# Transformer layer on one core: the fourth and later background tasks of a slot move between the two halves of its PV products

## The chip, the cores and the metric

One core of one Trainium2 chip runs the whole kernel as one launch. The metric is the device time of that launch in microseconds (us); lower is better. Before the change three runs gave 1093.54, 1095.59 and 1097.42 us, median 1095.59 us.

## The reference

The kernel computes one pre-norm layer on an input of 2048 tokens of width 128, all in float32: causal attention with 16 heads of width 64, then a mixture of eight experts (top 2) and one shared expert. Only the attention is touched. Cut to what matters:

```python
qkv = einsum('bse,ehd->bshd', layernorm(x), qkv_w) + qkv_b      # 16 heads, 3*64 each
logits = einsum('bqhd,bkhd->bhqk', q, k) / sqrt(64)             # causal mask: where(tril, logits, -big)
probs = softmax(logits)
attn = einsum('bhqk,bkhd->bqhd', probs, v)
x = x + einsum('bqhd,hde->bqe', attn, out_w) + out_b
x = x + shared_ffn(layernorm(x)) + routed_ffn(layernorm(x))     # 8 experts, top 2, hidden width 352
```

## The kernel before, in words

**Attention.** The 2048 queries of a head are four blocks of 512, its keys 16 tiles of 128. A *group* (b, p) is query block b against the two key tiles 2p and 2p+1, as far as the causal mask leaves any; there are 2+4+6+8 = 20 groups in a head (`GROUPS`), 320 in all. For a group TensorE (PE) computes the transposed scores into PSUM (`scores`, L827 and L828, and L832, which adds the mask on a diagonal tile), ScalarE (ACT) takes the exponential twice, once in float32 and once in float16 (L503, L504), GpSimd (POOL) subtracts the two to get the float16 remainder `p_lo` (L420), and PE multiplies both float16 parts with the values (`p_times_v`, L852, L854, L856). This last step is the "PV products": for each of the two key tiles (k = 0, 1) and each of up to four query tiles, three products of 64 or 65 columns in float16. So a full key tile gives 12 products and a diagonal one 3 to 12. The scores are products in float32 (`float32r`) of up to 512 columns.

**Slots.** PE's instructions are written out in one fixed order. Each head has 20 *slots*, one for each group. In slot n PE issues the first background task, the scores of the group's first key tile, the second background task, the scores of its second key tile, all the other background tasks of the slot, and then the PV products of the group three slots earlier (`LAG = 3`): first k = 0, then k = 1. Semaphore waits stand at the head of a product's weight load: the PV products of k = 0 wait for `p_lo`, and, where they begin a new query block, for `attn_ready`, by which VectorE (DVE) says that it has read the previous block's sums (`normalise`, L654 and L656). After k = 1 they count up `p_used`, which `normalise` and a later exponential wait for.

**Background tasks.** They prepare the next head and finish the last pair of heads, and all go through a ring of three PSUM banks `bg` (`BGRING = 3`): PE fills a bank, DVE drains it, and the task k waits until task k-3 is drained (`bg_drained`). The kinds are "qk" (three products of 512 columns, L743 to L745), "v" (L783), "att_t" (L803), "att_y" (L743 to L745), "shift" (L798), and "max": one float32 product of query tile t against key block c, 128 to 512 columns wide (L793), of which DVE takes the row maximum (L632, or L628 on the diagonal). The row maxima of a head are needed only at "shift", in slot 18 of the head before.

**The planner.** `background(h)` writes the slots at build time: fixed places for qk (slots 0 to 3), v, att_t, att_y and shift, and `fill` spreads the 40 max tasks of a head over the slots 4 to 17, by an estimate of what DVE needs for each. Run for all 16 heads, its lists have 83 slots with four tasks or more: 76 with four and 7 with five. By slot number these 83 are: slot 4 in 8 heads (in 7 of them with five tasks), slot 6 in 8, slot 7 in 14, slot 8 in 7, slot 10 in 6, slot 11 in 13, slot 12 in 6, slot 13 in 8, slot 14 in 13. The head 15 has none. Every fourth and fifth task is a "max": 90 tasks. In the 8 slots numbered 13 the third task is 128 columns wide and the fourth 512.

The ends of the order: before the slots a prologue prepares head 0 (until about 58 us of the span), head 15 runs from about 767 us, and a second layer norm and nine passes over expert weights end the kernel.

Of the kernel before, what the change touches and what calls it, by code (L numbers as in the profile page):

```python
# [52 lines left out]
def max_width(t, c):  # L53
    return min(BLK, P * (t + 1) - BLK * c)
# [26 lines left out]
def background(h):  # L81


    i, s = divmod(h, 2)
    slots = [[] for _ in range(NG)]
    if s == 0 and i:
        slots[ATT_LAST[0]].append(("att_t", i - 1, 3))
        slots[ATT_LAST[1]].append(("att_y", i - 1, 3))
    if s == 1:
        for b in range(NB - 1):  # L90
            slots[ATT_SLOTS[b][0]].append(("att_t", i, b))
            slots[ATT_SLOTS[b][1]].append(("att_y", i, b))
    if i + 1 < PAIRS:
        for k in range(2):
            slots[V_SLOTS[s][k]].append(("v", i + 1, 2 * s + k))
    if h + 1 < H:
        for b in range(NB):
            slots[b].append(("qk", h + 1, b))
        taken = [sum(map(vector_time, slot)) for slot in slots]
        for n in range(NG):  # L100
            if ends_block((n - LAG - 1) % NG):
                taken[n] += 0.6
        level = 1.5
        while True:
            trial = [list(slot) for slot in slots]
            if fill(trial, max_tasks(h + 1), [max(level - x, 0.1) for x in taken]):
                break
            level += 0.02
        slots = trial
        slots[SHIFT_SLOT].insert(0, ("shift", h + 1))  # L110
    return slots
# [5 lines left out]
SLOTS = [background(h) for h in range(H)]  # L117
# [6 lines left out]
def wait(eng, sem, value):  # L124

    if not isinstance(value, int) or value > 0:
        eng.wait_ge(sem, value)


def layer_kernel(nc, x_t, qkv_w, qk_bias_in, v_bias, out_w, out_bias, gate_w_t, ffn_w, out_t):  # L130
    ctx = ExitStack()
    with ctx:
# [129 lines left out]
        def blk(b):  # L262
            return slice(b * BLK, (b + 1) * BLK)

        def tile(t):
            return slice(t * P, (t + 1) * P)

        def drained(task):

            return NUMBER[task] + 1  # L270
# [469 lines left out]
        def _(pe):  # L740
            def mm3(out, w_hi_ap, w_lo_ap, x_hi_ap, x_lo_ap, start, stop, skip=False):

                nc.tensor.matmul(out, w_hi_ap, x_hi_ap, start=start, stop=False, skip_group_check=skip)  # L743
                nc.tensor.matmul(out, w_hi_ap, x_lo_ap, start=False, stop=False, skip_group_check=skip)  # L744
                return nc.tensor.matmul(out, w_lo_ap, x_hi_ap, start=False, stop=stop, skip_group_check=skip)  # L745
# [22 lines left out]
            def background_task(task):  # L768
                k = NUMBER[task]
                bank = bg[:, k % BGRING]  # L770
                wait(pe, bg_drained, k - BGRING + 1)
                if task[0] == "qk":
                    h, b = task[1:]
                    ws, s = h // 2 % 2, h % 2
                    if b == 0:
                        pe.wait_ge(w_lo_ready, h // 2 + 1)
                    mm3(bank, w_hi[ws][:, s], w_lo[ws][:, s], xn_hi[:, blk(b)], xn_lo[:, blk(b)], True, True
                        ).then_inc(bg_ready, 1)
                elif task[0] == "v":
                    i, q = task[1:]  # L780
                    pe.wait_ge(w_landed[i % 2], (i // 2 + 1) * 32)
                    for r in range(4):
                        mm = nc.tensor.matmul(bank[:, tile(r)], xn[:, tile(4 * q + r)], w_raw[i % 2][:, :, 2 * D:3 * D],  # L783
                                              start=True, stop=True)
                    mm.then_inc(bg_ready, 1)
                elif task[0] == "max":
                    h, t, c = task[1:]
                    s = h % 2
                    if t % 4 == 0 and c == 0:
                        pe.wait_ge(q_hi_landed[t // 4], (h + 1) * 32)  # L790
                        pe.wait_ge(k_lo_landed[t // 4], (h + 1) * 16)
                    width = max_width(t, c)
                    mm = nc.tensor.matmul(bank[:, 0:width], q_hihi[s][:, tile(t)],  # L793
                                          k_lohi[s][:, c * BLK:c * BLK + width], start=True, stop=True)
                    mm.then_inc(bg_ready, 1)
                elif task[0] == "shift":
                    pe.wait_ge(neg_max_ready, task[1] + 1)
                    nc.tensor.transpose(bank[0:NT, 0:P], neg_max[:], ident[:]).then_inc(bg_ready, 1)  # L798
                elif task[0] == "att_t":
                    i, b = task[1:]  # L800
                    pe.wait_ge(attn_ready, (i * 2 + 1) * NB + b + 1)
                    for r in range(4):
                        mm = nc.tensor.transpose(bank[:, tile(r)], attn[:, 4 * b + r, :], ident[:])  # L803
                    mm.then_inc(bg_ready, 1)
                elif task[0] == "att_y":
                    i, b = task[1:]
                    pe.wait_ge(wo_lo_ready, i + 1)
                    pe.wait_ge(bg_drained, drained(("att_t", i, b)))
                    mm3(bank, wo_hi[i % 2][:], wo_lo[i % 2][:], att_hi[:], att_lo[:], True, True).then_inc(bg_ready, 1)
# [27 lines left out]
            def p_times_v(h, n, k):  # L837

                b, p = GROUPS[n]
                B, (i, s) = h * NB + b, divmod(h, 2)  # L840
                if k == 0:
                    if n == 0 and s == 0:
                        pe.wait_ge(bg_drained, drained(("v", i, 3)))
                    if p == 0:
                        wait(pe, attn_ready, B)
                    pe.wait_ge(p_lo_ready, h * NG + n + 1)
                kt = 2 * p + k
                v = v_parts[i % 2][:, s, kt]
                for j in range(max(0, kt - 4 * b), 4):
                    out = pv4[:, j, :]  # L850
                    cols = slice(k * BLK + j * P, k * BLK + (j + 1) * P)
                    nc.tensor.matmul(out, p_hi[:, n % PRING, cols], v[:, 0:D + 1],  # L852
                                     start=(kt == 0 and j == 0), stop=False, skip_group_check=True)
                    nc.tensor.matmul(out[:, 0:D], p_hi[:, n % PRING, cols], v[:, D + 1:VW],  # L854
                                     start=False, stop=False, skip_group_check=True)
                    mm = nc.tensor.matmul(out, p_lo[:, n % PRING, cols], v[:, 0:D + 1],  # L856
                                          start=False, stop=(kt == 4 * b + j), skip_group_check=True)
                if k == 1:
                    mm.then_inc(p_used, 1)
# [15 lines left out]
            for h in range(H):  # L875
                for n in range(NG):
                    for task in SLOTS[h][n][0:1]:
                        background_task(task)
                    scores(h, n, 0)
                    for task in SLOTS[h][n][1:2]:  # L880
                        background_task(task)
                    scores(h, n, 1)
                    for task in SLOTS[h][n][2:]:
                        background_task(task)
                    m = (n - LAG) % NG
                    if m < n or h:
                        for k in range(2):
                            p_times_v(h if m < n else h - 1, m, k)
            for n in range(NG - LAG, NG):
                for k in range(2):  # L890
                    p_times_v(H - 1, n, k)
# [95 lines left out]
```

## Time and profile before

| | before |
|---|---|
| median of 3 runs | 1095.59 us |
| profiled execution, its own time | 1095.27 us |
| its span, first to last instruction | 1093.5 us |
| PE products (MATMUL) busy | 1050.8 us, 96% |
| PE weight loads (PEld) busy | 867.1 us, 79% |
| DVE, ACT, POOL busy | 799.5, 784.8, 757.2 us |
| TensorE clock granted, mean | 0.973 |

The rows below are from this one profiled execution. PE's products are pipelined, and the end of each is modelled: a row's duration is longer than the time until the next product may start. What the array really spends on a product is read from one start to the next; rows of the timeline give starts to 0.01 us. PEld is the weight load that precedes each product.

### The profile page before, as it was taken

Reading aid. Unit: us, or ns where it says so; the run is one execution under the profiler, and the core shown is the slowest. Engines: PE = TensorE matmul, PEld = TensorE weight load, DVE = VectorE, ACT = ScalarE, POOL = GpSimd, SP = SyncE. Lnnn points to the kernel's source line nnn. Section 1 sums busy time; section 2 is a strip of 40 time slices with the busy share of each in tenths; the row PEclk is TensorE's granted clock in tenths of the full one; section 3 lists DMA queues with packets and bytes.
Section 4 is the critical chain, followed back from the end, with each engine's and each line's share of the span. In section 5 each row is a group of like instructions: output and inputs, shape, how many; then the busy total and the mean of one; then the engine's idle time right before and its main releaser. Section 6 shows DMA issues by size and latency. Waiting matters only on the chain.

```text
span 1093.5 us, 25737 instructions
## 1 busy us (share of the span) xinstructions
PE 1050.8 (96%) x10580; PEld 867.1 (79%) x10580; DVE 799.5 (73%) x1659; ACT 784.8 (72%) x952; POOL 757.2 (69%) x427
## 2 busy tenths in 40 slices
PE   7889999999999999999999999999976999999998
PEld 5478888888888888888888888888855677777776
DVE  5976878787787878778787787878225577777765
ACT  3068787878878787887878888788952656666664
POOL 2058878888878887887888788788970556555540
PEclk9689999999999999999999999999986999999999
DMA  2330312303032130312303031130100311111001
GB/s 83 67 78 6 75 38 50 79 2 86 11 69 61 26 80 2 86 25 56 71 16 79 2 86 38 44 75 6 46 1 1 107 76 61 60 60 60 39 1 38
DMA packets 24653, 53.22 MB, mean 49 GB/s; under 512 B 5720, under 2 KB 8024, under 8 KB 22488
## 3 DMA queue, kind: packets, MB, share of 16 engines
q1 hardware_dynamic: 24544, 51.68, 18.3%
q8 instruction: 80, 1.31, 0.5%
q14 instruction: 29, 0.24, 0.1%
HBM read 16.86 MB, written 1.11 MB: 16 GB/s over the span
## 4 chain that ended last, share of the span: by engine, by line
PE 71%; POOL 11%; issue 6%; DVE 5%; DMA 4%; ACT 2%; SPq 0%; POOLq 0%; ACTq 0%; DVEq 0%
PE bg L793 13%; PE st L827 11%; PE st L828 11%; PE pv L852 6%; PE pv L854 6%; PE pv L856 6%; POOL xw L442 4%; POOL p_lo L420 3%; PE bg L743 3%; DMA attn<-comb_dram 3%; PE bg L783 2%; POOL k_lohi L447 2%; PE bg L744 2%; PE bg L745 2%; POOL q_lo_shift L434 2%
## 5 line engine op out<-in xcount | busy, mean ns | idle before, releaser
L420 POOL TENSOR_TENSOR p_lo<-prob,p_hi 128x1024 f16<-128x1024 f32 x320 | 617.1, 1946 | 156.3 <-ACT p_hi L504 154.5
L503 ACT ACTIVATE prob<-st,p_bias 128x1024 f32<-128x1024 f32 x320 | 330.3, 1032 | 126.5 <-PE st L828 100.5
L504 ACT ACTIVATE p_hi<-st,p_bias 128x1024 f16<-128x1024 f32 x320 | 328.4, 1026 | 0.0
L632 DVE TENSOR_REDUCE row_max<-bg 128x1 f32<-128x512 f32 x384 | 255.6, 686 | 16.0 <-PE bg L793 10.8
L827 PE MATMUL st<-q_hihi,k_lohi 128*128 128x512 f32 (+3 forms) x640 | 245.7, 384 | 2.7 <-DMA q_lo_shift<-shift_row 1.4
L852 PEld LDWEIGHTS pv<-v_parts,p_hi 128*128 128x128 f16 x2176 | 197.6, 96 | 58.0 <-issue 39.4
L793 PE MATMUL bg<-k_lohi,q_hihi 128*128 128x512 f32 (+3 forms) x640 | 239.9, 406 | 3.4 <-DVE v_parts L622 2.1
L852 PE MATMUL pv<-v_parts,p_hi 128*128 128x65 f16 x2176 | 236.2, 194 | 2.2 <-POOL p_lo L420 2.2
L828 PE MATMUL st<-q_lo_shift,k_hi_one 65*128 65x512 f32 (+3 forms) x640 | 235.6, 368 | 0.0
L854 PE MATMUL pv<-v_parts,p_hi 128*128 128x64 f16 x2176 | 233.7, 195 | 0.0
L856 PE MATMUL pv<-v_parts,p_lo 128*128 128x65 f16 x2176 | 231.9, 192 | 0.0
L856 PEld LDWEIGHTS pv<-v_parts,p_lo 128*128 128x128 f16 x2176 | 202.9, 99 | 0.0
L854 PEld LDWEIGHTS pv<-v_parts,p_hi 128*128 128x128 f16 x2176 | 202.6, 97 | 0.0
L793 PEld LDWEIGHTS bg<-k_lohi,q_hihi 128*128 128x128 f32 x640 | 122.0, 194 | 29.7 <-DVE row_max L632 7.7
L827 PEld LDWEIGHTS st<-q_hihi,k_lohi 128*128 128x128 f32 x640 | 122.4, 191 | 17.7 <-ACT p_hi L504 2.3
L828 PEld LDWEIGHTS st<-q_lo_shift,k_hi_one 65*128 65x128 f32 x640 | 121.7, 190 | 16.7
L727 DVE TENSOR_TENSOR prob<-prob,st 128x512 f32<-128x512 f32 x108 | 73.9, 684 | 72.9 <-ACT prob L548 72.4
L548 ACT ACTIVATE prob<-st 128x512 f32<-128x512 f32 x108 | 64.5, 597 | 67.0 <-PE st L745 67.0
L612 DVE TENSOR_SCALAR k_lohi<-bg,qk_bias 128x512 fp32r<-128x512 f32 x64 | 48.0, 750 | 72.4 <-PE bg L745 72.3
L442 POOL TENSOR_TENSOR xw<-xn,attn 128x512 f32<-128x512 f32 x32 | 51.2, 1611 | 62.3 <-DMA attn<-comb_dram 61.0
L628 DVE CUSTOM_DVE_ANT_0 xw<-bg,mask_wide 128x512 f32<-128x512 f32 (+2 forms) x169 | 79.0, 474 | 7.6 <-PE bg L793 7.4
L434 POOL TENSOR_TENSOR q_lo_shift<-e_raw,k_hi_one 128x1152 fp32r<-128x1152 f32 x9 | 24.8, 2750 | 60.5 <-ACT k_hi_one L527 60.5
(147 smaller groups left out, 1643.8 us busy)
## 6 DMA issues: line engine op xcount, KB each, us to landing
q_hihi<-k_lohi SPq DMA_DIRECT2D x128, 128.0 KB, 2.3
k_lohi<-q_lo_shift SPq DMA_DIRECT2D x64, 128.0 KB, 2.3
k_hi_one<-k_lohi SPq DMA_DIRECT2D x16, 512.0 KB, 4.3
attn<-comb_dram SPq DMA_DIRECT2D x8, 1024.0 KB, 4.4
e_raw<-ffn_w SPq DMA_DIRECT2D x9, 576.0 KB, 5.4
w_raw<-qkv_w SPq DMA_DIRECT2D x8, 192.0 KB, 2.3
res<-x_t SPq DMA_DIRECT2D x4, 256.0 KB, 3.8
out_t<-xn SPq DMA_DIRECT2D x4, 256.0 KB, 2.5
```

What stands on the lines that cost most here:

```text
L420: nc.gpsimd.tensor_tensor(o, a, b, ALU.subtract).then_inc(p_lo_ready, 1)
L442: nc.gpsimd.tensor_tensor(xw32[:, b % 2], xn[:, blk(b)], w_tok[:, blk(b)], ALU.mult).then_inc(xw_ready, 1)
L503: nc.scalar.activation(o32, src, ACT.Exp, bias=p_bias[:], scale=D ** -0.5)
L504: nc.scalar.activation(o16, src, ACT.Exp, bias=p_bias[:], scale=D ** -0.5).then_inc(exp_done, 1)
L628: nc.vector.tensor_tensor_reduce(masked[k % BGRING][:, 0:width], bank[:, 0:width], mask_wide[:, BLK - width:BLK], 1.0, -3.0e38, ALU.add, A ...
L632: nc.vector.tensor_reduce(row_max[:, t, c:c + 1], bank, AX_X, ALU.max).then_inc(bg_drained, 1)
L793: mm = nc.tensor.matmul(bank[:, 0:width], q_hihi[s][:, tile(t)], k_lohi[s][:, c * BLK:c * BLK + width], start=True, stop=True)
L827: nc.tensor.matmul(out, k_lohi[s][:, tile(kt)], q_hihi[s][:, q], start=True, stop=False)
L828: mm = nc.tensor.matmul(out, k_hi_one[s][0:D + 1, tile(kt)], q_lo_shift[s][0:D + 1, q], start=False, stop=not diagonal)
L852: nc.tensor.matmul(out, p_hi[:, n % PRING, cols], v[:, 0:D + 1], start=(kt == 0 and j == 0), stop=False, skip_group_check=True)
L854: nc.tensor.matmul(out[:, 0:D], p_hi[:, n % PRING, cols], v[:, D + 1:VW], start=False, stop=False, skip_group_check=True)
L856: mm = nc.tensor.matmul(out, p_lo[:, n % PRING, cols], v[:, 0:D + 1], start=False, stop=(kt == 4 * b + j), skip_group_check=True)
```

## The change

In each slot the tasks from the fourth on are issued between the PV products of k = 0 and those of k = 1, and no longer ahead of both. A slot with three tasks or fewer keeps its order. DVE, ACT, POOL and the DMA queue keep their programs: DVE drains the banks in the same order as before, since the order of the background tasks among themselves is unchanged.

```diff
                     scores(h, n, 1)
-                    for task in SLOTS[h][n][2:]:
+                    for task in SLOTS[h][n][2:3]:
                         background_task(task)
                     m = (n - LAG) % NG
                     if m < n or h:
-                        for k in range(2):
-                            p_times_v(h if m < n else h - 1, m, k)
+                        p_times_v(h if m < n else h - 1, m, 0)
+                    for task in SLOTS[h][n][3:]:
+                        background_task(task)
+                    if m < n or h:
+                        p_times_v(h if m < n else h - 1, m, 1)
```

## Rows read from the trace of the kernel before

**Rows 1.** The page: share of the span and instructions; the chain that ended last.
```profile
PE 1050.8 (96%) x10580; PEld 867.1 (79%) x10580; DVE 799.5 (73%) x1659; ACT 784.8 (72%) x952; POOL 757.2 (69%) x427
PE 71%; POOL 11%; issue 6%; DVE 5%; DMA 4%; ACT 2%; SPq 0%; POOLq 0%; ACTq 0%; DVEq 0%
```
**Rows 2.** Windows, all engines (stretch, its length, busy us of each, PEclk, DMA share, GB/s).
```profile
320.00:384.00 64.00, 64.00 (x777) 54.19 (x775) 52.52 (x116) 51.35 (x54) 52.03 (x29) 1.00 0.16 38
...
64.00:767.20 703.20, 702.56 (x8701) 597.57 (x8701) 553.83 (x1246) 577.50 (x612) 582.88 (x312) 1.00 0.21 48
```
**Rows 3.** Waits of the weight loads, 109 to 755 us (us in total, times, longest).
```profile
PEld pv L852 <- issue: 33.4, 147, 0.3
PEld pv L852 <- POOL p_lo L420: 8.8, 34, 0.3
PEld bg L793 <- DVE row_max L628: 0.3, 1, 0.3
```
**Rows 4.** Waits of the weight loads for drained max banks, whole span.
```profile
PEld bg L793 <- DVE row_max L632: 7.7, 22, 0.5
...
PEld bg L793 <- DVE row_max L628: 2.8, 10, 0.5
```
**Rows 5.** Timeline of PE, head 5, slot 11 and the start of slot 12 (start, us).
```profile
323.06 0.27 PE L832 MATMUL st<-mask_cols_r,ident_r 128*128 128x128 f32 x1
323.17 0.67 PE L793 MATMUL bg<-k_lohi,q_hihi 128*128 128x512 f32 x2
323.69 0.20 PE L852 MATMUL pv<-v_parts,p_hi 128*128 128x65 f16 x1
...
323.79 0.19 PE L852 MATMUL pv<-v_parts,p_hi 128*128 128x65 f16 x1
...
324.07 0.19 PE L852 MATMUL pv<-v_parts,p_hi 128*128 128x65 f16 x1
...
324.43 0.48 PE L743 MATMUL bg<-att_hi,wo_hi 128*128 128x512 f32 x1
324.75 0.39 PE L744 MATMUL bg<-att_lo,wo_hi 128*128 128x512 f32 x1
324.98 0.40 PE L745 MATMUL bg<-att_hi,wo_lo 128*128 128x512 f32 x1
```
**Rows 6.** Products of the qk tasks, whole span (count, busy us, mean ns of one).
```profile
L743 PE MATMUL bg<-xn_hi,w_hi 128*128 128x512 f32 x64 | 30.9, 482 | 0.9 <-DVE xn_lo L584 0.5 <-DVE q_lo_shift L614 0.4
L744 PE MATMUL bg<-xn_lo,w_hi 128*128 128x512 f32 x64 | 25.8, 403 | 0.0
```
**Rows 7.** Timeline of PE, head 5, first task of slot 4, which follows PV products.
```profile
304.43 0.31 PE L793 MATMUL bg<-k_lohi,q_hihi 128*128 128x128 f32 x1
304.57 0.45 PE L827 MATMUL st<-q_hihi,k_lohi 128*128 128x512 f32 x1
```
**Rows 8.** Timeline of PE, head 7, slot 4 and the start of slot 5.
```profile
400.54 0.85 PE L793 MATMUL bg<-k_lohi,q_hihi 128*128 128x384 f32 x3
...
401.50 0.19 PE L856 MATMUL pv<-v_parts,p_lo 128*128 128x65 f16 x1
401.59 1.16 PE L783 MATMUL bg<-w_raw,xn 128*128 128x128 f32 x8
```
**Rows 9.** Timeline of DVE, the same stretch.
```profile
400.97 0.56 DVE L628 CUSTOM_DVE_ANT_0 xw<-bg,mask_wide 128x384 f32<-128x384 f32 x1 [0.21 <-PE bg L793]
401.45 0.08 DVE L628 DVE_READ_ACCUMULATOR2_ANT row_max<- 128x1 f32 x1
```
**Rows 10.** Timeline of PE, head 5, slot 13, third and fourth task.
```profile
329.51 0.51 PE L793 MATMUL bg<-k_lohi,q_hihi 128*128 128x128 f32 x2
```
**Rows 11.** Timeline of DVE, head 5, slots 13 and 14.
```profile
330.11 0.69 DVE L632 TENSOR_REDUCE row_max<-bg 128x1 f32<-128x512 f32 x1
331.03 1.39 DVE L632 TENSOR_REDUCE row_max<-bg 128x1 f32<-128x512 f32 x2 [0.23 <-PE bg L793]
```
**Rows 12.** Timeline of POOL, head 5, groups 8 and 9.
```profile
318.79 4.24 POOL L420 TENSOR_TENSOR p_lo<-prob,p_hi 128x1024 f16<-128x1024 f32 x2 [0.96 <-ACT p_hi L504]
```

## The prediction

> **What bounds the kernel now.** I read the page first. PE's products are busy for 96% of the span and PE holds 71% of the chain that ended last; no other engine has more than 11% of it [rows 1]. A busy share is an average over stages, and PE's ends are modelled, so the windows come next. In a stretch of attention PE is busy for all 64.00 of 64.00 us, with the clock at 1.00, while DVE has 52.52, ACT 51.35 and POOL 52.03; over all the slots of heads 0 to 14 it is 702.56 of 703.20 us [rows 2]. The reader is to see that nothing but PE's own stream can be late there by much. The waits say the same. Between 109 and 755 us the weight loads waited for a drained max bank once, for 0.3 us [rows 3]; the larger sums for the whole span, 7.7 and 2.8 us [rows 4], therefore belong nearly all to the prologue, where PE fills banks as fast as DVE drains them. The two big entries, 33.4 and 8.8 us before the first PV load, are 181 pieces of at most 0.3 us, 0.23 us on average [rows 3]. The timeline shows what they are: the PV load stands behind a running float32 product of 512 columns, and the PV product starts when that product's turn is over. It is PE work beside an idle load port and not lost time.
>
> So the change is to be priced on PE's stream, from start to start. A float32 product of 512 columns behind another wide one takes 0.23 us (324.75 to 324.98), and a full key tile of PV products 0.38 us for 12 (323.69 to 324.07) [rows 5].
>
> **The change part by part.** No instruction is added or removed; 90 max products in 83 slots move behind the PV products of k = 0. What changes are PE's neighbours. Before: ... third, fourth, PV0, PV1, next slot. After: ... third, PV0, fourth (and fifth), PV1, next slot. The stream now goes from float16 products to a float32 product once more in each of the 83 slots, and from float32 to float16 once more.
>
> (1) *Float16 to float32, a cost.* The first float32 product after PV products takes 0.32 us to the next start (324.43 to 324.75), against 0.23 for the one behind it [rows 5]. Over all 64 qk tasks the first product has 482 ns, the second 403, so 79 ns more [rows 6]; most of these first products stand behind PV products. A narrow one pays the same: 128 columns, which at the wide product's pace are 0.06 us, took 0.14 (304.43 to 304.57) behind PV products [rows 7]. The load of float32 weights is longer than the 0.03 us for which a PV product covers it, so its tail lies open. I take 0.08 us. The exact case, a max product behind PV products with its bank drained long before, is in the trace already at the head of slots such as this one. 83 x 0.08 = 6.6 us.
>
> (2) *Float32 to float16, a cost.* The first three PV products after a float32 one take 0.10 us (323.69 to 323.79), against 0.38 / 12 x 3 = 0.095 in the whole tile [rows 5]. Rounded starts allow 0 to 0.02; the longer spans of first products that I looked at favour 0.01. 83 x 0.01 = 0.8 us.
>
> (3) *The narrow neighbour, a gain.* A wide product behind a 128-column one also pays for an open load: third and fourth task behind a mask product took 0.52 us (323.17 to 323.69), which is 0.29 + 0.23 [rows 5]. In the 8 slots numbered 13 the third task is 128 columns wide and the fourth 512 [rows 10]. There this 0.06 goes, since a PV product follows the narrow one: -8 x 0.06 = -0.5 us.
>
> (4) *The bank wait of slot 5, a gain.* In the 7 slots with five tasks the first task of the next slot needs the bank of the third. DVE's last step on that bank is over at 401.45 + 0.08 = 401.53, and PE starts the next task at 401.59, 0.09 after the last PV product instead of 0.03 [rows 8, 9]. With slot 4 itself 0.09 longer, PE comes after the drain: -7 x 0.06 = -0.4 us. The other bank waits of moved tasks are not there to be saved, by the 0.3 us in all [rows 3].
>
> (5) *POOL, nothing.* The PV products of k = 0 come earlier by one max product, 0.23 us, and their wait for `p_lo` with them. In slot 11 of head 5 group 8 is wanted at 323.69 [rows 5]; POOL did groups 8 and 9 in one run from 318.79 to 323.03, so group 8 was ready at about 320.9 [rows 12]: 2.8 us of cover, of which 0.23 goes. `p_used` comes 0.09 us later with the rest of the stream, and ACT, POOL and the loads of the next head are paced by the scores, which keep their place. SP's queue issues nothing inside the moved block.
>
> (6) *DVE, nothing by my reading.* A moved task's bank lands later by PV0 plus the switch, at most 0.38 + 0.09 = 0.47 us. DVE starts 0.43 us after the start of a product when it has been waiting (400.54 to 400.97) [rows 8, 9]. In slot 13 it started the fourth 0.54 us after that product's start (329.57 to 330.11), a backlog of 0.11; the delay for DVE is then 0.36 + 0.07 - 0.06 - 0.11, about 0.3 us [rows 10, 11]. But DVE waits 0.23 us for the next slot's first task there [rows 11], which absorbs it, and the moved bank is wanted again only by the third task after it. In slot 4 with five tasks DVE begins the fourth at 401.53 at the latest, and the fourth product would start at about 400.98 instead of 400.77: no delay.
>
> The sum is 6.6 + 0.8 - 0.5 - 0.4 = 6.5 us. It is on PE's stream in the stretch where nothing else is last, so it moves everything behind it; the head 15, whose end waits for POOL, has no moved task and cannot hide any of it. The profiled execution took 1095.27 us (span 1093.5 and 1.8 outside): 1095.27 + 6.5 = 1101.8. The median of the three runs is 0.3 higher, so I forecast 1102.1 us, 0.6% slower.
>
> *A rule of the Trainium skill that speaks against (1).* The rows show 0.32 against 0.23 us [rows 5]. "TensorE: Matmul & The Clock Gate", section "Step-by-step: what each phase is for", says that TensorE pulls a weight load ahead of the products in flight, so that the next weights load while the current product runs. Taken as full cover, the switch is free and the sum would be -0.5 - 0.4, no change; the rows say that a PV product is too short a cover.
>
> **The rivals.**
> *A. The switch is hidden, no change.* If the load of the moved product is issued early enough behind PV0 (its bank is long free, unlike a slot's first task in some cases), the 0.08 shrinks. For it: the load port has idle time. Against: the qk and max tasks at slot heads, whose banks are also free, pay 0.08 as a rule [rows 5 to 7]. From full to no cover the time is 1094.7 to 1102.1; with half of it 6.5 - 3.3 = 3.2, 1098.8.
> *B. Faster: the ring of three banks.* The fourth task needs the first's bank, and 0.38 us of PV products now stand in front of it. If the 10.5 us of waits for drained max banks [rows 4] lay in these slots, they would go: 1095.6 - 10.5 + 6.5 = 1091.6. It decides as soon as a moved task waited over 0.09 us before. Against: 0.3 us in the stretch that holds nearly all of them [rows 3].
> *C. Slower by more: DVE late.* If the 0.3 us of slot 13 reaches PE (through the next slot's banks or `attn_ready`), 8 slots cost another 0.2 each beyond PE's own delay, and some 0.06 in the 13 slots 14: 1.6 + 0.8 = 2.4, 1104.5. For it: slot 4 to 5 of head 7 shows that such a chain can be tight [rows 8, 9]. Against: DVE's slack of 11 us in 64 [rows 2] and the 0.23 us of waiting right behind.
> *D. POOL late for the earlier PV products.* If the 34 pieces put down to `p_lo` [rows 3] were real waits, moving them up costs 34 x 0.23 = 7.8: 1109.9. Against: the 2.8 us of cover.
>
> **How the numbers follow.** This kernel's runs differ by up to 0.2% from their median, so about 0.3%, 3.3 us, is what a measurement can tell from no change. Chances: the forecast with its bounds (switch 0.06 to 0.10 in all, 1099.7 to 1103.0, and 1.5 us of measurement on either side) 0.80; A 0.10, mostly inside 0.3%; B 0.03; C 0.05; D 0.02. Faster 0.04, same 0.11, slower 0.85. The range, 1098.5 to 1105.5, takes in C and the upper half of A, and leaves out B, D and the free switch.
>
> **What would show it.** In the changed profile: a moved max product of 512 columns takes 0.31 to 0.32 us to the next start behind PV0 (0.23: A is right); PE still busy for 64.00 of 64.00 us; heads 0 to 14 longer by about 6.5 us and the rest unchanged; the 0.2 to 0.3 us pieces of idle load port before the first PV load grow in number by about 83, of the k = 1 half; waits for `attn` and for `row_max` in 109 to 755 us no larger (larger: C), those for `p_lo` no longer than 0.3 each (longer: D). The prediction is wrong if the time moves without PE's start-to-start intervals around the moved products doing so.

## The result, and the profile after

The changed kernel took 1105.14 us (median of 4 runs, 1104.52 to 1106.62) against 1095.83 for the kernel before, a ratio of 1.0089, 95% interval 1.0068 to 1.0109. Timed again beside the experiments it took 1104.51 against 1097.57, a ratio of 1.0063 (1.0045 to 1.0082). It is slower by 7 to 9 us, where 6.5 us, a ratio of 1.0059, were forecast: inside the second interval and below the first. 1105.14 us lies in the forecast's range, near its upper edge.

The page of the changed kernel answers to [rows 1]: PE holds the same share of the chain, and its busy time has grown by 11.1 us.

```profile
PE 1061.9 (96%) x10580; PEld 870.9 (79%) x10580; DVE 804.7 (73%) x1659; ACT 785.4 (71%) x952; POOL 757.6 (69%) x427
PE 71%; POOL 11%; issue 6%; DVE 5%; DMA 4%; ACT 2%; SPq 0%; POOLq 0%; ACTq 0%; DVEq 0%
```

The stages say where. These are windows as in [rows 2], cut at the first product of slot 0, the first score product of head 15 and the last PV product: first the kernel before, then the changed one.

```profile
0.00:30.00 30.00, 22.14 (x117) 16.99 (x117) 17.88 (x28) 9.36 (x18) 9.05 (x20) 0.94 0.34 92
30.00:57.41 27.41, 22.48 (x58) 12.30 (x58) 26.46 (x65) 0.00 (x0) 0.00 (x0) 0.69 0.22 48
57.41:767.60 710.19, 708.10 (x8723) 602.02 (x8722) 556.28 (x1249) 579.90 (x614) 583.27 (x312) 1.00 0.21 48
767.60:810.00 42.40, 38.92 (x579) 32.55 (x579) 8.63 (x17) 39.45 (x43) 42.09 (x24) 0.99 0.07 25
810.00:1093.40 283.40, 259.14 (x1111) 203.20 (x1108) 190.24 (x301) 156.04 (x278) 122.80 (x73) 0.95 0.13 49
```
```profile
0.00:30.00 30.00, 24.36 (x101) 19.29 (x101) 15.07 (x24) 9.37 (x18) 7.98 (x20) 0.77 0.26 74
30.00:60.18 30.18, 24.84 (x75) 14.13 (x74) 29.39 (x69) 0.00 (x0) 1.07 (x1) 0.72 0.28 62
60.18:777.47 717.29, 715.62 (x8723) 602.01 (x8722) 560.26 (x1249) 580.56 (x614) 583.92 (x312) 1.00 0.21 48
777.47:819.70 42.23, 38.72 (x579) 32.37 (x579) 8.64 (x17) 39.45 (x43) 41.89 (x24) 1.00 0.07 26
819.70:1102.70 283.00, 258.33 (x1113) 203.09 (x1109) 191.35 (x301) 156.03 (x278) 122.79 (x73) 0.95 0.13 49
```

The span is 9.2 us longer. Heads 0 to 14 have 7.1 of it (717.29 - 710.19), with the same number of products and the clock at 1.00 in both. The other 2.8 us lie ahead of the first slot, where the two programs issue the same instructions: the mean granted clock of the first 30 us was 0.94 in the one execution and 0.77 in the other. Head 15 and all behind it gave back 0.6.

The traces can be cut finer, at the first product of each slot. Here are heads 1 to 14, changed kernel less the kernel before, once for the two first profiles and once for the second profile of the changed kernel (after_again) less that of the unedited copy (control).

| slots of heads 1 to 14 | number | grew by, us, first pair | second pair |
|---|---|---|---|
| four tasks, not slot 13 | 66 | 6.37 | 6.33 |
| slot 13, four tasks, third one 128 columns wide | 7 | 0.34 | 0.35 |
| slot 13 of head 14, four tasks, third one 512 wide | 1 | 0.09 | 0.09 |
| five tasks (slot 4) | 7 | 0.27 | -0.22 |
| all others, nothing moved | 199 | 0.10 | -0.62 |

The growth sits in the slots with a moved task, 0.097 us by the median of the 66, and hardly anywhere else. Two profiles of the same program differ too: heads 0 to 14 took 1.66 us more in the copy than in the kernel before, but 1.6 of that lie in four single slots, numbered 3 or 4. Differences of whole stretches below about 2 us therefore say little, and differences slot by slot say much more. (The paragraph on the planner, and term (3) of the forecast, give all 8 slots numbered 13 a narrow third task. It is so in 7: in head 14 the second task is the narrow one.)

The timeline of PE in slot 11 of head 5 answers to [rows 5].

```profile
328.13 0.28 PE L828 MATMUL st<-q_lo_shift,k_hi_one 65*128 65x128 f32 x1
328.24 0.27 PE L832 MATMUL st<-mask_cols_r,ident_r 128*128 128x128 f32 x1
328.35 0.44 PE L793 MATMUL bg<-k_lohi,q_hihi 128*128 128x512 f32 x1
328.63 0.20 PE L852 MATMUL pv<-v_parts,p_hi 128*128 128x65 f16 x1
...
328.99 0.19 PE L856 MATMUL pv<-v_parts,p_lo 128*128 128x65 f16 x1
329.01 0.48 PE L793 MATMUL bg<-k_lohi,q_hihi 128*128 128x512 f32 x1
329.34 0.20 PE L852 MATMUL pv<-v_parts,p_hi 128*128 128x65 f16 x1
...
329.69 0.19 PE L856 MATMUL pv<-v_parts,p_lo 128*128 128x65 f16 x1
329.71 0.48 PE L743 MATMUL bg<-att_hi,wo_hi 128*128 128x512 f32 x1
```

From the third task to the next slot's first product are 1.36 us (328.35 to 329.71) instead of 1.26 (323.17 to 324.43). The moved product takes 0.33 to the next start instead of 0.23. Over the 57 moved fourth tasks of 512 columns this interval has a median of 0.321 us.

The waits of the weight loads between 111 and 760 us answer to [rows 3].

```profile
PEld pv L852 <- issue: 40.5, 186, 0.3
PEld pv L852 <- POOL p_lo L420: 5.9, 22, 0.3
PEld pv L852 <- DVE attn L656: 1.6, 6, 0.3
```

The view of [rows 3] has the same line for `attn`, between its second and its third:

```profile
PEld pv L852 <- DVE attn L656: 1.6, 6, 0.3
```

There is no wait for a row maximum. The pieces of idle load port ahead of PV loads are 208 instead of 181, where the forecast looked for 83 more. In total the port's idle time ahead of L852 is 68.1 us instead of 58.0, in the page's table of costliest groups, so it did grow by about 0.12 us a slot, but most of it in pieces that this view does not list. That sign of the forecast failed; it had named the wrong view for it.

### The profile page after: what moved, and what is told of

It reads as the page before. It is cut to its first block, busy times and chain, and to the rows that moved or that the text cites. A ratio compares the mean times of both kernels' runs of the same rounds, so it can differ in the third digit from the quotient of the medians.

```text
span 1102.7 us, 25737 instructions
## 1 busy us (share of the span) xinstructions
PE 1061.9 (96%) x10580; PEld 870.9 (79%) x10580; DVE 804.7 (73%) x1659; ACT 785.4 (71%) x952; POOL 757.6 (69%) x427
## 4 chain that ended last, share of the span: by engine, by line
PE 71%; POOL 11%; issue 6%; DVE 5%; DMA 4%; ACT 2%; SPq 0%; POOLq 0%; ACTq 0%; DVEq 0%
PE bg L793 13%; PE st L827 11%; PE st L828 11%; PE pv L852 6%; PE pv L854 6%; PE pv L856 5%; POOL xw L442 4%; POOL p_lo L420 3%; DMA attn<-comb_dram 3%; PE bg L743 3%; POOL k_lohi L447 2%; PE bg L783 2%; PE bg L744 2%; PE bg L745 2%; POOL q_lo_shift L434 2%
## 5 line engine op out<-in xcount | busy, mean ns | idle before, releaser
L632 DVE TENSOR_REDUCE row_max<-bg 128x1 f32<-128x512 f32 x384 | 255.8, 686 | 18.2 <-PE bg L793 12.8
L793 PE MATMUL bg<-k_lohi,q_hihi 128*128 128x512 f32 (+3 forms) x640 | 258.6, 415 | 3.3 <-DVE v_parts L622 2.1
L852 PEld LDWEIGHTS pv<-v_parts,p_hi 128*128 128x128 f16 x2176 | 197.2, 96 | 68.1 <-issue 47.2
L827 PE MATMUL st<-q_hihi,k_lohi 128*128 128x512 f32 (+3 forms) x640 | 245.8, 384 | 2.5 <-ACT p_hi L504 1.6
L852 PE MATMUL pv<-v_parts,p_hi 128*128 128x65 f16 x2176 | 245.4, 195 | 2.2 <-POOL p_lo L420 2.2
L854 PE MATMUL pv<-v_parts,p_hi 128*128 128x64 f16 x2176 | 242.2, 195 | 0.0
L856 PE MATMUL pv<-v_parts,p_lo 128*128 128x65 f16 x2176 | 240.1, 192 | 0.0
L827 PEld LDWEIGHTS st<-q_hihi,k_lohi 128*128 128x128 f32 x640 | 122.4, 191 | 18.2 <-ACT p_hi L504 2.8
L828 PEld LDWEIGHTS st<-q_lo_shift,k_hi_one 65*128 65x128 f32 x640 | 121.7, 190 | 16.7
L434 POOL TENSOR_TENSOR q_lo_shift<-e_raw,k_hi_one 128x1152 fp32r<-128x1152 f32 x9 | 24.8, 2752 | 59.2 <-ACT k_hi_one L527 59.2
```

The source lines that it names most:

```text
L632: nc.vector.tensor_reduce(row_max[:, t, c:c + 1], bank, AX_X, ALU.max).then_inc(bg_drained, 1)
L827: nc.tensor.matmul(out, k_lohi[s][:, tile(kt)], q_hihi[s][:, q], start=True, stop=False)
L828: mm = nc.tensor.matmul(out, k_hi_one[s][0:D + 1, tile(kt)], q_lo_shift[s][0:D + 1, q], start=False, stop=not diagonal)
```

## Experiments

Each kernel was timed in five rounds beside the kernel before. "Heads 0 to 14" is read in its profiled execution between the same two products as above. The kernel before has 710.19 us in its first profile, its copy 711.85.

| run | ratio to before, 95% interval | heads 0 to 14, us |
|---|---|---|
| control (before, a copy) | 1.0003 (0.9992 to 1.0015) | 711.85 |
| after_again (the change) | 1.0063 (1.0045 to 1.0082) | 717.76 |
| fourth_behind | 1.0020 (1.0007 to 1.0033) | 712.21 |
| third_between | 1.0124 (1.0106 to 1.0141) | 726.91 |
| scores_between | 1.0120 (1.0099 to 1.0141) | 723.01 |
| third_behind | 1.0128 (1.0107 to 1.0149) | 725.13 |
| diagonal_behind | 1.0043 (1.0024 to 1.0062) | 715.72 |
| covered | 1.0085 (1.0067 to 1.0103) | 720.66 |
| beside | 1.0139 (1.0116 to 1.0163) | 725.58 |
| pairs | 1.0098 (1.0079 to 1.0116) | 718.97 |
| pairs_shift | 1.0146 (1.0126 to 1.0166) | 722.78 |
| pairs_spread | 1.0270 (1.0247 to 1.0293) | 742.10 |

The theory is the forecast's: what costs is that PE changes once more from float16 to float32 products, 0.08 us, and back, 0.01, in each of the 83 slots (the switch). The main rival, L, is that the moved tasks reach DVE late and the delay comes back to PE.

**control and after_again: the start.** No edit.

> The kernel before, unedited, as a second copy. The changed kernel was 9.3 us slower, but its heads 0 to 14 only 7.1 us; 2.8 us more lay ahead of the first slot (first slot at 60.2 us instead of 57.4), at a lower granted clock. Theory P1 (start by chance): the time to the first slot varies from one execution to the next by 2 us or more, at different clocks, in this kernel too; the ratio is 1.000. Theory P2 (the start belongs to the program): this copy reaches its first slot at 57.4 us within 0.5 us.

> The changed kernel, unedited, timed beside the others. Switch theory: heads 0 to 14 take 7.1 us more than before again. P1: the first slot starts anywhere between 56 and 61 us, and the whole is slower by 6.5 to 7.1 us plus or minus what the start differs. P2: the first slot starts at 60.2 us within 0.5 us and the whole is 9.3 us slower.

The copy reached its first slot at 59.4 us, against 57.4 in the first profile. The windows of its first 30 us and of the stretch behind the last PV product:

```profile
0.00:30.00 30.00, 23.89 (x106) 18.18 (x107) 15.96 (x25) 9.36 (x18) 8.70 (x20) 0.83 0.29 80
...
813.40:1099.80 286.40, 261.81 (x1115) 205.24 (x1111) 191.13 (x301) 156.06 (x278) 123.13 (x73) 0.94 0.13 48
```

P1 holds: with identical instructions ahead of it, the first slot began between 57.4 and 60.8 us over the 14 profiled executions (12 different kernels), and what follows the last PV product took 283.1 to 287.3. The kernel before alone ran from 1095.49 to 1101.17 us in 23 runs of one session. The changed kernel reached its first slot at 59.2 us this time, and the difference to before was 6.9 us, with 717.76 us in heads 0 to 14.

**fourth_behind: no extra switch, and the banks later still.** Against the changed kernel:

```diff
                     if m < n or h:
-                        p_times_v(h if m < n else h - 1, m, 0)
+                        for k in range(2):
+                            p_times_v(h if m < n else h - 1, m, k)
                     for task in SLOTS[h][n][3:]:
                         background_task(task)
-                    if m < n or h:
-                        p_times_v(h if m < n else h - 1, m, 1)
```

> The fourth and fifth tasks of a slot stand behind both halves of the PV products. Switch theory: PE goes from float16 to float32 as often as in the kernel before, since the next slot begins with float32 anyway, so heads 0 to 14 take the time of before, within 0.5 us. Theory L (the moved tasks reach DVE late, and that delay comes back to PE): DVE gets them later still, by up to 0.75 us instead of 0.47, so heads 0 to 14 are slower than in the changed kernel, by over 7 us against before.

Heads 0 to 14 took 712.21 us, 0.4 more than the copy of before and 2.0 more than its first profile. The later banks do show as waits:

```profile
PEld pv L852 <- DVE attn L656: 4.7, 20, 0.3
PEld bg L783 <- DVE row_max L628: 1.8, 7, 0.3
PEld bg L793 <- DVE row_max L632: 1.2, 7, 0.2
```

These are its load waits between 110 and 755 us. `attn` has 20, against 6 in the kernel before and in the changed one, and two kinds of bank waits are new. But with the switches gone most of the 7 us are gone, although DVE gets the tasks later than in the changed kernel; L asked for more than 7. The total is 0.2% over before, by an interval that leaves out 1. Whether these waits make it or the scatter of starts and ends is not shown.

**third_between: twice the switches.** Against the changed kernel:

```diff
-                    for task in SLOTS[h][n][2:3]:
-                        background_task(task)
...
-                    for task in SLOTS[h][n][3:]:
+                    for task in SLOTS[h][n][2:]:
```

> Already the third task stands between the two halves of the PV products, in all 173 slots that have one, instead of 83. Switch theory: 173 extra switches in each direction at 0.08 + 0.01 us, less 0.05 for each of the 52 narrow products that no longer stand ahead of a float32 one: 13.0 us more than before in heads 0 to 14. Theory L: the delay of each bank is what counts; banks of third tasks are drained with the same slack as fourth ones, so the cost grows with the 173 to at least 7.1 x 2.1 = 14.8 us, with waits of PE for drained banks or attn of over 1 us in all.

Heads 0 to 14 took 15.1 us more than the copy, 16.7 more than the first profile. This run does not decide between the theories. The switches make 13.0 by the forecast's price, and L had asked for at least 14.8 us with waits of over 1 us, which are there: `attn` 26 times with 7.4 us of idle load port, and 1.9 us for `row_max`. Cut by slots, the 161 slots of heads 1 to 14 with a third task grew by 14.5 us against the copy, 0.096 by the median, and most of them lie near 0.05 (narrow neighbours) or 0.1; only slot 9 has 0.15 on average. That is what a fixed price with some waits on top looks like, but it is the next run that tells the two apart.

**scores_between: switches without any task moved.** Against the kernel before, cut to the new lines:

```diff
+                    early = values and h < H - 1 and len(SLOTS[h][n]) <= 2
+                    if early:
+                        p_times_v(h if m < n else h - 1, m, 0)
                     scores(h, n, 1)
...
```

> No background task moves. In the 124 slots of heads 0 to 14 with at most two tasks, the scores of the second key tile stand between the two halves of the PV products. Switch theory: 124 extra switches in each direction at 0.09 us, less 0.05 for each narrow product that no longer stands ahead of a float32 one, 8.3 us in all, and the rows show 0.31 to 0.32 us from the start of the first score product behind PV0 to the next. Theory L (late banks at DVE are what costs): no bank comes later against its neighbours than before, so heads 0 to 14 take the time of before within 1 us.

Heads 0 to 14 grew by 11.2 to 12.8 us, where L says under 1. The timeline shows the price at the moved products, 0.31 us to the next start and 0.23 behind it:

```profile
311.01 0.19 PE L856 MATMUL pv<-v_parts,p_lo 128*128 128x65 f16 x1
311.04 0.48 PE L827 MATMUL st<-q_hihi,k_lohi 128*128 128x512 f32 x1
311.35 0.39 PE L828 MATMUL st<-q_lo_shift,k_hi_one 65*128 65x512 f32 x1
311.58 0.20 PE L852 MATMUL pv<-v_parts,p_hi 128*128 128x65 f16 x1
```

By the forecast's prices 8.3 us are the 124 switches. The trace puts the growth where the switches are: the 119 slots of heads 1 to 14 with at most two tasks took 10.8 us more than in the copy, the other 161 slots 0.0. The median of the 119 is 0.086 us. Eight slots numbered 5 hold 2.4 us of it, up to 0.39 each; they begin a query block, and `attn` is waited for 13 times here (3.9 us of idle load port) instead of 6. A wait for a transfer of `k_lohi` also shows.

**third_behind and diagonal_behind: the narrow neighbours, and a try at a faster kernel.** Tasks from the third on behind both halves, in all slots or only where the second scores end with a mask product (the condition in this diff, cut to its end, which third_behind lacks), against the kernel before:

```diff
+                    if diagonal:
+                        for task in SLOTS[h][n][2:]:
+                            background_task(task)
```

> The third and all later tasks stand behind both halves of the PV products, in 173 slots. Switch theory: as many switches as in the kernel before; only narrow products that stood ahead of a float32 one now stand ahead of PV products, 45 x 0.05 = 2.2 us less in heads 0 to 14, minus what new waits for attn in slot 5 take (0.14 us in each odd head with the fourth task behind): -2.2 to 0 us. Theory L: slower than before by over 2 us, since every bank in these slots comes later by 0.3 to 0.75 us.

> A version meant to beat both kernels: only in the slots whose second scores end with a mask product (52 slots with three tasks or more) do the third and later tasks stand behind both halves of the PV products. Switch theory: the mask product of 128 columns then stands ahead of PV products, which need no open float32 load: 52 x 0.05 = 2.6 us less in heads 0 to 14, no extra switch. Theory L: slower, by 0.3 us or more in each of the slots, or no gain.

Both failed: -2.2 to 0 and -2.6 us were expected. There is no additional switch, yet heads 0 to 14 took 725.13 and 715.72 us, 13.3 and 3.9 more than in the copy. The load waits of third_behind between 110 and 782 us name the place:

```profile
PEld pv L852 <- DVE attn L656: 10.6, 29, 0.5
PEld bg L793 <- DVE row_max L632: 9.6, 33, 0.4
...
PEld bg L783 <- DVE row_max L628: 3.8, 6, 0.6
```

These are idle times of the load port and not lost time one for one. Third, fourth and the next slot's tasks now stand close together, and a ring of three banks lets PE run at most three tasks ahead of DVE. So L names a true limit of this kernel, and the change stayed on the free side of it. That the waits make the whole 13.3 us is argued from their size; no run takes them away alone.

**covered and beside: what the 0.08 us are.** One more float16 product of 252 columns in each of the 83 slots of the changed kernel, ahead of the moved tasks (covered) or behind them (beside). The diff is that of beside, against the changed kernel:

```diff
+                    if SLOTS[h][n][3:]:
+                        nc.tensor.matmul(pv[:, 260:512].rearrange("p (a c) -> p a c", a=2),
+                                         p_hi[:, m % PRING, 3 * P:4 * P],
+                                         v_parts[(h if m < n else h - 1) // 2 % 2][:, 0, 0:2, 0:126],
+                                         start=False, stop=False, skip_group_check=True)
```

> The changed kernel with one more float16 product of 252 columns in each of its 83 slots, between PV0 and the moved task; it writes PSUM columns that nobody reads. The question is what the 0.08 us of the switch are. Open-load theory: the float32 load takes about 0.11 us and only the product before it covers it; behind a product of 0.107 us (252 columns at the pace of a PV product's 65 in 0.029) it is covered, so the pair costs 0.107 - 0.08 = 0.03 us a slot: heads 0 to 14 take 717.5 + 2.4 = 719.9 us, and the moved product takes 0.23 us to the next start. Fixed-price theory (each change of type costs 0.08 whatever stands before it): 717.5 + 83 x 0.107 = 726.4 us, and the moved product takes 0.31 to 0.32.

> The same extra product of 252 columns, but behind the moved tasks, as the first of the k = 1 half, where it covers only a float16 load. Both theories: 83 x 0.107 = 8.9 us more than the changed kernel in heads 0 to 14, 726.4 us, and the moved product still takes 0.31 to 0.32 us to the next start. It is the price of the product alone, for comparison with the run before.

Against after_again the same product cost 7.8 us behind the moved tasks (725.58 - 717.76) and 2.9 ahead of them (720.66 - 717.76); by the ratios 8.3 and 2.4. So about 5 of its 8 us vanish where a float32 load follows, as the open-load theory said. Slot by slot, where the scatter drops out, it is clearer: over the 66 slots with four tasks the product cost 0.105 us behind the moved task and 0.032 ahead of it, so 0.073 of the switch's 0.08 are hidden. A price of the change of type that is paid whatever stands ahead of it is ruled out. That it is the weight load which is covered, and not some other delay of the same length, is supported by products that change no type: of 128 columns each and all float32, they stand 0.11 us apart (328.13, 328.24 and 328.35 in the changed kernel's slot 11), where one of 128 columns behind a wide float32 product takes 0.06 by the median.

But the row that both theories pointed to did not behave. Here is PE at a moved task of 128 columns in the covered kernel, and at one of 512 columns in beside:

```profile
320.90 0.19 PE L856 MATMUL pv<-v_parts,p_lo 128*128 128x65 f16 x1
320.93 0.27 PE L889 MATMUL pv<-v_parts,p_hi 128*128 128x252 f16 x1
320.96 0.31 PE L793 MATMUL bg<-k_lohi,q_hihi 128*128 128x128 f32 x1
321.11 0.21 PE L852 MATMUL pv<-v_parts,p_hi 128*128 128x65 f16 x1
```
```profile
320.62 0.48 PE L793 MATMUL bg<-k_lohi,q_hihi 128*128 128x512 f32 x1
320.94 0.28 PE L891 MATMUL pv<-v_parts,p_hi 128*128 128x252 f16 x1
321.06 0.19 PE L852 MATMUL pv<-v_parts,p_hi 128*128 128x65 f16 x1
```

The product of 252 columns takes 0.12 us to the next start in beside, and 0.03 in covered, where the float32 product behind it still takes its long 0.15 (0.14 in [rows 7]); over all 64 moved tasks of 512 columns in covered it is 0.32, not the 0.23 expected. The record starts the float32 product 0.03 us after whatever float16 product stands before it. So at a switch a single start-to-start interval is not the time of one product; the sum over the switch is what counts, and 0.03 + 0.32 is the 0.105 of this product and the 0.23 of the next, within 0.02.

**pairs, pairs_shift, pairs_spread: half the switches.** The PV products of two groups together, in even slots only. pairs_shift issues slot 18's background tasks behind them; pairs_spread also the fourth and fifth tasks of the even slots. The diff is that of pairs, against the kernel before:

```diff
-                    m = (n - LAG) % NG
-                    if m < n or h:
-                        for k in range(2):
-                            p_times_v(h if m < n else h - 1, m, k)
-            for n in range(NG - LAG, NG):
+                    if n % 2 == 0:
+                        for m in (n - 4, n - 3):
+                            if m >= 0 or h:
+                                for k in range(2):
+                                    p_times_v(h if m >= 0 else h - 1, m % NG, k)
+            for n in range(NG - 4, NG):
```

> The kernel before with the PV products of two groups issued together, in even slots only (groups n-4 and n-3 in slot n). PE goes from float16 to float32 158 times instead of 316. Switch theory: 158 x 0.09 = 14.2 us less, and narrow neighbours give back 1.2: 13 us less, 697 us for heads 0 to 14, if no new wait arises. Theory L (banks and scores late at DVE and ACT bound the order): tasks and scores of two slots now follow one another without PV products in between, and PE waits for drained banks or for exp as in the kernel with all later tasks behind; then over half of the 13 us are lost, and it may be slower than before.

> The kernel with PV products in pairs of groups, and in slot 18 its background tasks (the shift, which waits for the last row maximum) behind the PV products. In the paired kernel the shift's wait took 8.8 of the 20 us by which heads 1 to 14 were longer than their products ask. If the rest stays, 719.0 - 8.8 = 710 us for heads 0 to 14: the kernel before, no gain. If the waits for banks shrink too once DVE is less behind, down to 705. If the later shift row makes the next head's first scores wait (its DMA takes 1.9 us), 712 or more.

> As pairs_shift, and in the even slots the fourth and fifth tasks stand behind the PV products. No switch is added. If late banks at DVE are what eats the gain of the halved switches, the PV products between the third and the fourth task give DVE up to 0.75 us and heads 0 to 14 take 2 to 5 us less than pairs_shift. If it only moves the crowd of tasks into the next slot, the same or more.

No version beats the kernel before. The load waits of pairs between 111 and 776 us:

```profile
PEld bg L798 <- DVE row_max L628: 12.3, 14, 1.1
PEld bg L793 <- DVE row_max L632: 10.4, 34, 0.4
...
PEld bg L743 <- DVE row_max L632: 2.9, 7, 0.4
```

These are 25.6 us of idle load port. Heads 0 to 14 took 718.97 us, where 697 were expected if no wait arose: the new waits cost about 20 us, more than the 13 saved. With the shift behind the PV products its wait is gone, but the next head's scores find ACT late (11.6 us of idle load port ahead of L827 for `p_hi`), and the sum is higher; spreading the tasks made it worse still, where 2 to 5 us less had been one expectation and the same or more the other. By slots, slot 0 of heads 1 to 14, with those scores, took 13.5 us more in pairs_shift than in pairs and 17.8 us more in pairs_spread. The rest of the 23 us between pairs_spread and pairs is not separated.

## Why the prediction was right in its mechanism, and off in size

**What bounds the kernel.** Right. The stretch stayed dense in PE, and the only engine whose program changed is the one that got longer.

**(1) and (2), the switch.** Right, slightly too small. 0.09 us a slot were put in. The 66 slots with four tasks outside slot 13 grew by 0.097 each by the median, and slot 11 of head 5 shows 0.10 (1.36 against 1.26). Over 83 slots that is 0.6 us more than forecast. scores_between shows that the price needs no background task, and covered against beside that most of it can be hidden behind a longer product.

The Trainium skill ("TensorE: Matmul & The Clock Gate", "Step-by-step: what each phase is for") says that the next weights load while the current product runs. Covered against beside agrees, with 0.073 us hidden behind the longer product. The forecast was right not to read it as full cover: behind a product of 65 columns the switch still cost 0.097.

**(3), the narrow neighbour.** The gain is there, smaller and in one slot fewer. Seven slots 13 have a narrow third task, and they grew by 0.048 us instead of 0.097: 0.05 each, not 0.06, and 0.3 us in all instead of 0.5. Slot 13 of head 14, without it, grew by 0.09. The kernels built to collect more of this gain lost it to waits.

**(4), the bank wait of slot 5.** Right in place and size. Five of the seven slots with five tasks grew by 0.03 us in both pairs of profiles, 0.09 less 0.06; the other two, in heads 5 and 11, scatter by more than that. Behind it a small wait moved. DVE is done with `attn` in head 7 at 408.87 + 0.42 = 409.29 us, and PE, no longer held up by the bank, now comes to it a little too early: from the mask product to the first PV product are 0.15 us (409.20 to 409.35), where before there were 0.12. The slot as a whole did not get longer by it: slot 5 changed by -0.01 us in the sum of the seven odd heads.

```profile
408.87 0.42 DVE L656 TENSOR_TENSOR attn<-pv,rden 128x256 f32<-128x256 f32 x1
```
```profile
409.20 0.27 PE L832 MATMUL st<-mask_cols_r,ident_r 128*128 128x128 f32 x1
409.35 0.20 PE L852 MATMUL pv<-v_parts,p_hi 128*128 128x65 f16 x1
```

**(5) and (6), POOL and DVE.** Right. The waits for `p_lo` stayed at 0.3 us at the longest, no wait for a row maximum appeared, and those for `attn` are 6, as before. DVE met the moved task of slot 11 at 329.53, 0.52 us after its product's start, without a stall at PE.

**The rivals.** A (the switch hidden) is out by the slot's own rows. B (faster by the ring of banks) is out: there was nothing to save, as [rows 3] said. C did not happen here: the slots 14, for which it had a delay, grew by 0.096 like the others. It is the limit that fourth_behind touches and third_behind and pairs run into. D did not happen.

**How the numbers followed: the step that failed.** The 6.5 us were sound: heads 0 to 14 grew by 7.1 us, of which 0.6 are the switch at 0.097 instead of 0.09. What failed is the step from there to a time, "How the numbers follow": the base of 1095.59 us, the median of three runs (1095.27 of the profiled one and 0.3), and the 1.5 us allowed for measurement on either side of 1099.7 to 1103.0. 1105.14 lies 2.1 above 1103.0.

The runs showed a wider scatter. In four later sessions the kernel before took 1095.49 to 1101.17 us in 56 runs, with medians from 1097.40 to 1098.61; none of the 56 was as fast as the fastest of the first three, 1093.54. The changed kernel repeated its time, 1104.51 after 1105.14. So the base was some 2 us too low for this kernel, and against 1097.57 the difference is 6.9. The profiles show where such scatter arises. The one behind the forecast had the earliest start of the 14, 57.4 us to the first slot. The stage ahead of the slots moves by 3.4 us from one execution to the next, and the stage behind the last PV product by 4.2. Of the 9.2 us by which the two first spans differ, 7.1 are in heads 0 to 14, 2.8 are the start, and -0.6 the end. Why the first session had so fast a kernel before is not known; four runs are few, and it may be chance.

## What to carry to other kernels

On an engine with no gaps, moving work costs what its new neighbours cost: here 0.1 us each time a float32 product stands behind a float16 one of 65 columns, which is too short to cover its weight load. Count the changes of type in the order before moving anything, and price a move over the whole switch, never by one interval. Look at several runs for the base of a forecast before you give it 1.5 us of room, and compare two profiles slot by slot, where the scatter of the ends drops out. And where a ring of few banks feeds another engine, fewer switches bought by crowding its tasks are paid back with interest.

## What the runs showed of the hardware

A float16 product of 252 columns cost 0.105 us a slot ahead of a float16 load (beside less after, 66 slots) and 0.032 ahead of a float32 load (covered less after): 0.07 us of the load's length were hidden. The same product's row shows 0.12 and 0.03 us to the next start.

The mean clock granted in the first 30 us took four values in 14 executions with the same instructions there. With 0.94 the first slot began at 57.4 to 58.3 us (five executions), with 0.89 at 58.0 to 59.4 (four), with 0.83 at 58.9 to 59.9 (three), and with 0.77 at 60.2 and 60.8. What decides which it is, no run here shows.
